# Where the attention's output bias is added: by GpSimd on each image, or by TensorE inside the output projection

## What is computed

```python
def _L0_attn_ref(x, W_qkv, b_qkv, W_o, b_o):
    qkv = x @ W_qkv.T + b_qkv
    ...
    probs = jax.nn.softmax(scores / sqrt(hd), axis=-1)
    out = jnp.einsum('bkhd,bhqk->bqhd', V, probs)
    out = out.reshape(B, S, H)
    return out @ W_o.T + b_o

h = _L0_tok_ref(x, ...)                                   # weighted sum over 4 groups
h = h + _L0_attn_ref(_layernorm(h, axis=-1), W_qkv, b_qkv, W_o, b_o)
h = h + _L0_ffn_ref(_layernorm(h, axis=-1), ...)          # 64 experts, 6 per token, and a shared one
```

## Time and profile before

| | |
|---|---|
| median of 3 runs | 524.37 us (523.19 to 525.21) |
| span of the profiled execution | 527.1 us |
| PE, DVE, ACT, POOL busy over the span | 88%, 63%, 53%, 46% |
| mean granted TensorE clock | 0.953 of full speed |
| POOL's bias add, L397 | 16 of them, 724 to 766 ns each |
| image loop, first to last bias add | 25.0 to 230.3 us |

### The profile page before, as it was taken

How to read it: one execution, slowest core, us unless ns; L and a number is a source line. 1 busy time by engine, 2 the same in 40 slices (tenths; PEclk the granted TensorE clock), 3 DMA queues, 4 the chain that set the end, 5 groups by cost and what they waited for, 6 DMA issues and landing times. The chain is left out here.

```text
span 527.1 us, 11459 instructions
## 1 busy us (share of the span) xinstructions
PE 463.1 (88%) x2974; PEld 351.2 (67%) x2974; DVE 331.5 (63%) x1065; ACT 278.4 (53%) x902; POOL 244.1 (46%) x273
## 2 busy tenths in 40 slices
PE   1687989999999999987648999999999999996796
PEld 1556666766666776755225888888888888873564
DVE  4682658998999999888661443444444444440897
ACT  3285778888777888873201444444445544440000
POOL 1111110566555666666770565665655665661000
PEclk9996989999999999998776999999999999998899
DMA  8999930111111111112224559667678566652997
GB/s 275 348 347 309 299 99 2 61 63 60 62 63 61 62 62 61 63 70 81 101 100 114 181 171 291 203 188 241 200 209 270 165 209 212 205 157 65 415 390 282
DMA packets 56471, 89.82 MB, mean 170 GB/s; under 512 B 7719, under 2 KB 43690, under 8 KB 56400
## 3 DMA queue, kind: packets, MB, share of 16 engines
q1 hardware_dynamic: 44016, 61.62, 37.5%
q0 software_dynamic: 10080, 25.29, 13.6%
q10 hardware_dynamic: 2304, 2.10, 1.1%
HBM read 83.93 MB, written 40.82 MB: 237 GB/s over the span
## 5 line engine op out<-in xcount | busy, mean ns | idle before, releaser
L419 POOL DMA_INDIRECT y_rows<-y,xring x114 | 112.1, 984 | 90.8 <-issue 82.8
L1048 PE MATMUL ps<-wring,prob 128*128 x456 | 119.7, 386 | 0.0
L1009 DVE TENSOR_TENSOR probt<-probt,ps 128x128 f32<-128x128 f32 x114 | 32.8, 288 | 108.6 <-issue 90.7
L1048 PEld LDWEIGHTS ps<-wring,prob 128*128 128x128 f32 x456 | 79.4, 194 | 6.3
L474 ACT ACTIVATE prob<-ps,nmax 128x128 f32<-128x128 f32 x256 | 69.7, 391 | 4.1 <-DVE nmax L706 3.3
L572 ACT COPY prob<-ps 128x256 f32<-128x256 f32 x115 | 42.8, 372 | 48.6 <-PE ps L1279 48.3
L1048 PE MATMUL ps<-wring,probt 128*128 x228 | 68.2, 381 | 0.0
L577 ACT ACTIVATE probt<-ps 128x128 f32<-128x128 f32 x114 | 31.6, 277 | 58.3 <-PE ps L1048 58.3
L1002 DVE TENSOR_SCALAR y<-ps,xring 128x256 f32<-128x256 f32 x114 | 54.6, 479 | 5.8 <-DMA y_rows<-y,xring 4.6
L389 POOL DMA_INDIRECT slot_rows<-row,slot_ix x48 | 50.7, 1056 | 13.7 <-issue 13.4
L389 POOL DMA_INDIRECT slot_rows<-xring,slot_ix x48 | 50.4, 1050 | 14.0 <-issue 13.7
(11 more groups left out here) (173 smaller groups left out, 790.2 us busy)
## 6 DMA issues: line engine op xcount, KB each, us to landing
wring<-wexp SPq DMA_DIRECT2D x115, 384.0 KB
xring<-slot_rows SPq DMA_DIRECT2D x115, 129.0 KB, 2.3
x_sb<-y_rows SPq DMA_DIRECT2D x16, 768.0 KB, 6.3
slot_rows<-pads SPq DMA_DIRECT2D x1, 8256.0 KB, 33.9
x_sb<-x SPq DMA_DIRECT2D x3, 2048.0 KB, 17.8
slot_rows<-pads SPq DMA_DIRECT2D x5, 516.0 KB, 9.6
x_sb<-x SPq DMA_DIRECT2D x4, 512.0 KB, 5.1
out<-h_all ACTq DMA_DIRECT2D x16, 128.0 KB, 6.6
```

The costliest lines, as they stand in the source:

```text
L419: nc.gpsimd.indirect_dma_start(out=y_dram, out_offset=bass.IndirectOffsetOnAxis(ap=xring[:, q, TO_AT:TO_AT + 1].bitcast(I32), axis=0), in_ ...
L1009: nc.vector.tensor_tensor(hm[:, t % 2, :], silu[:, t % 2, :], psS[t % 2][:, INTER:2 * INTER], ALU.mult).then_inc(S("h_ready"), 1)
L1048: return nc.tensor.matmul(*a, **k)
```

## The change

POOL's add per image goes, and with it the semaphore `bias_added` and DVE's wait for it. Once, after `bias_joined`, POOL makes three bf16 terms whose sum is the f32 bias (the first is its rounding, the next two round what is left), multiplies each by a column that is 1 in partition 0, 1 or 2 alone, and adds them up into `bo_rows`, a bf16 tile in which partitions 0, 1 and 2 hold the three terms and all others hold zero. TensorE then starts each projection with one matmul of a matrix of ones and `bo_rows`, which adds the three rows up in every output row, and goes on with the projection's own matmuls in the same accumulation.

```diff
+            split(nc.gpsimd.tensor_copy(bo_term[:, 0, :], bo_sb[:]), 1)
+            split(nc.gpsimd.tensor_tensor(bo_rest[:, 0, :], bo_sb[:], bo_term[:, 0, :], ALU.subtract), 2)
+            split(nc.gpsimd.tensor_copy(bo_term[:, 1, :], bo_rest[:, 0, :]), 3)
+            split(nc.gpsimd.tensor_tensor(bo_rest[:, 1, :], bo_rest[:, 0, :], bo_term[:, 1, :], ALU.subtract), 4)
+            split(nc.gpsimd.tensor_copy(bo_term[:, 2, :], bo_rest[:, 1, :]), 5)
+            for k in range(3):
+                split(nc.gpsimd.tensor_scalar(bo_term[:, k, :], bo_term[:, k, :], c("term")[:, k:k + 1], None,
+                                              ALU.mult), 6 + k)
+            split(nc.gpsimd.tensor_tensor(bo_term[:, 0, :], bo_term[:, 0, :], bo_term[:, 1, :], ALU.add), 9)
+            nc.gpsimd.tensor_tensor(bo_rows[:], bo_term[:, 0, :], bo_term[:, 2, :], ALU.add).then_inc(
+                S("bias_rows"), 1)
...
-                if has(v):
-
-                    pool.wait_ge(S("ln1_done"), v + 1)
-                    nc.gpsimd.tensor_tensor(h_all[:, v, :], h_all[:, v, :], bo_sb[:], ALU.add).then_inc(
-                        S("bias_added"), 1)
...
-                    dve.wait_ge(S("bias_added"), cc + 1)
...
-                    both(psC[:, D:2 * D], lambda k: ont[:, k, :], lambda k: wo_sb[:, k, :]).then_inc(
-                        S("proj_done"), 1)
+                    if cc == 0:
+                        pe.wait_ge(S("bias_rows"), 1)
+                    mm(psC[:, D:2 * D], ones_b[:], bo_rows[:], start=True, stop=False)
+                    for k in range(KT):
+                        last = mm(psC[:, D:2 * D], ont[:, k, :], wo_sb[:, k, :], start=False, stop=k == KT - 1)
+                    last.then_inc(S("proj_done"), 1)
```

More of the change, by code:

```diff
@@ L53 @@
 C_AT = {}
-for _name, _n in (("ident", P), ("causal", P), ("before", P), ("half", 2), ("ebase", E),
+for _name, _n in (("ident", P), ("causal", P), ("before", P), ("half", 2), ("term", 3), ("ebase", E),
                   ("dest", NB * TOPK), ("spill", 1 + NY), ("upto", E), ("tile", NTAB)):
@@ L103, in build @@
         bo_sb = sb("bo_sb", [P, D])
+        bo_rest = sb("bo_rest", [P, 2, D])
+        bo_term = sb("bo_term", [P, 3, D], BF16)
+        bo_rows = sb("bo_rows", [P, D], BF16)
         gate_sb = sb("gate_sb", [P, KT, E])
@@ L223, in build @@
                      "prob_transposed", "probt_ready", "pv_done", "ot_ready", "ot_turned", "c2_chain", "o_ready",
-                     "o_transposed", "ont_ready", "bias_added", "proj_done", "ln_chain", "x2_ready", "var_ready", "root_ready", "var_eps", "half_set",
+                     "o_transposed", "ont_ready", "bias_split", "bias_rows", "proj_done", "ln_chain", "x2_ready", "var_ready", "root_ready", "var_eps", "half_set",
                      "x2_transposed", "x2t_ready", "gate_done", "gate_tanh", "g_chain", "score_read", "sel_ready",
@@ L382, in _, with split @@
             pool.wait_ge(S("bias_joined"), 1)
+            def split(ins, n):
+                ins.then_inc(S("bias_split"), 1)
+                pool.wait_ge(S("bias_split"), n)
+            split(nc.gpsimd.tensor_copy(bo_term[:, 0, :], bo_sb[:]), 1)
[9 more added lines that the diff above has]
+                S("bias_rows"), 1)
             def step(b, par):
-                v, e = b + 1, b - 3
+                e = b - 3
                 def scatter(choices):
@@ L1365 @@
     put("half", p[:, None] // HD % 2 == np.arange(2)[None, :])
+    put("term", p[:, None] == np.arange(3)[None, :])
     put("ebase", np.arange(E)[None, :] * REGION + P + 1)
```

## The result

The changed kernel took 522.86 us (median of 13 runs, 518.38 to 525.21), the kernel before 525.31 us (13 runs, 523.19 to 529.04). The ratio, taken between runs made side by side, is 0.9939, with a 95% interval of 0.9913 to 0.9965. That is 3.2 us less (1.8 to 4.6; the two medians differ by 2.45), a little more than the 0.5% that a measurement can tell. The forecast of 1.1 us less had the sign right and the size too small; the time lies inside the range. In the two profiled executions the span went from 527.1 to 522.1 us.

A forecast was written before the change was run, and what follows sets the result against it. Mid-loop PE and DVE are nearly always busy, and POOL's add holds DVE, delaying ACT's exponential. Terms -1.8 - 0.4 + 0.4 + 0.2 + 0.5 = -1.1 us took 524.37 to 523.3 us; range 520.3 to 526.9.

The forecast's parts named there:

- Where the time goes: Image loop: POOL's add stalls DVE 2.7 us at L731 and L751, making ACT's exponential 3.0 us late over eleven steps.
- 0.21 to 0.58: DVE's stalls per step in us, taken as about as large as the exponential's lateness of 0.20 to 0.78.
- The steady part, -1.8: Eleven loop steps: 3.0 us gained by removing the add, less 1.2 for the new matmul on turn(3).
- second-order gain: PE's 1.6 us of waits for DVE's o_sb in the loop: a quarter, 0.4 us, counted as gained.
- The price of 0.11: Cost in us of each new 256-column matmul on PE ahead of turn(3), bounds 0 and 0.21.
- The start, +0.5: POOL's split from 24.96 us, 6.2 us long, slows DVE's mixing of the third image: 0.5 us lost.
- the start costs its upper bound: Rival: each of four mixing instructions at the start waits out a POOL instruction, 2.6 us lost; 525.4 us, chance 0.15.
- PE's clock falls at the start: Rival: PE idles and returns at half clock in the 10 us behind 30.26, 2.5 us more; 527.9 us, chance 0.12.
- The first three projections, +0.4: Around 59, 75 and 88 us the exponential is not late, so the matmul is pure cost: 0.4 us lost.
- The end, +0.2: At 242.60 us DVE idles for a projection that the matmul delays by 0.11, or 0.22 at half clock: 0.2 lost.
- The rival in which the stall returns whole and the matmul is free: Rival: all of DVE's stalls and PE's o_sb waits come back, matmul hidden in PE's pauses; -3.8 us, 520.6 us, chance 0.18.
- The base: Starting time of 524.37 us for the kernel before, from which the forecast's 1.1 us was taken.

The follow-up runs named there:

- e1: The kernel before without POOL's add and without any output bias, no split and no matmul of ones; ratio to before 0.9950, steps 126.96 us.
- e9: The kernel before with POOL's add moved whole from ahead of the roots to behind them; ratio to before 0.9961, steps 128.82 us.
- e6: The kernel before with each POOL add made twice, the first into a spare tile; ratio to before 1.0032, steps 130.23 us.
- e7: The kernel before with each POOL add replaced by a fill of a spare tile, bias left out; ratio to before 0.9954, steps 128.28 us.
- e2: The kernel before with POOL's add kept and the new matmul put in, on rows of zeros; ratio to before 0.9978, steps 129.35 us.
- e4: The changed kernel with three more matmuls of ones on rows of zeros per projection; ratio to before 1.0027, steps 129.34 us.
- e3: The kernel before with the add kept and POOL's split of the bias made at the start, read by nobody; ratio to before 0.9999, steps 129.46 us.
- e5: The changed kernel with the whole projection, new matmul included, moved behind turn(3); ratio to before 0.9953, steps 126.77 us.
- e10: The changed kernel with DVE's maximum of group 0 made ahead of the choice of experts; ratio to before 0.9928, steps 125.87 us.

## Why the prediction was right or wrong, point by point

- **Where the time goes.** Right. L731 and L751 went back to 225 and 171 ns, the exponential stands 0.48 us behind the copy in all eleven steps, and e1, e9 and e6 show the add as the cause, by way of whom it holds. The stall was not at these two lines alone: "0.21 to 0.58" a step is misread, since in two steps neither is held and the exponential is 0.2 us late by L807. The 3.0 us of lateness, from which the sum was made, had L807's part in it, so the term stood.
- **The steady part, -1.8.** The sum is right, with its second-order gain of 0.4: -2.2 forecast for eleven steps, -2.10 measured over ten. Its terms are not, and that they cancel is in part luck. Taking the add away gave 2.46 us (e1) where I had 3.0, since PE then waited more for `o_sb`; the matmul took back 0.36 (after against e1) where I had 1.2 less 0.4. The account closes within 0.2: lateness -3.0, wait for `o_sb` -0.4, ten matmuls by 0.11 on PE +1.1, in all -2.3. (*Late* counts eleven exponentials; the first, 0.2 us late, stands ahead of the ten steps.) It closes for e1 too (-3.0 + 0.4 = -2.6; -2.46 measured), for e9 (-0.6; -0.60), for e7 (-1.6 + 0.5 = -1.1; -1.14) and for e6 (+0.7; +0.81), and roughly for e2 (-1.4 + 1.1 = -0.3; -0.07). It doesn't for e4: 3.3 - 1.6 = 1.7, and 2.0 was measured. The price of 0.11 was halved from wider matmuls and met exactly. "By 0.1 to 0.2 us a step" was 0.21.
- **The start, +0.5.** Wrong; of the mis-sized terms it moved the forecast most, as those of the steady part cancel. The split lasted 7.7 us, nearer the upper bound of 8.4 than my 6.2, and yet cost 0: I took a price for DVE's mixing from one overlap, but the mixing took 1.84 us beside the casts and two-input steps of the split, as it took 1.87 beside the add. The 0.34 that one overlap had cost was paid before as well, and none came on top. With it the rivals *the start costs its upper bound* and *PE's clock falls at the start* fell: the exponential they needed late came on time (30.28), and e3 gives 0.9999 for the split alone.
- **The first three projections, +0.4.** Too high. The last copies of these images start at 59.83, 75.59 and 88.59 us where they started at 59.79, 75.58 and 88.47: about 0.1 in all, and the roots at 104 are no later. What met the rest of the matmul's cost there I haven't traced.
- **The end, +0.2.** Wrong in kind. In place of 0.2 lost the traces show 1.24 gained, but this is where a stretch of half clock lay in the execution before, and the other traces show it with and without the change. What the change itself costs there these two traces can't show.
- **The rival in which the stall returns whole and the matmul is free, 520.6.** It fell: e2 against e1 and after shows that it is free only while the add's stall covers it, and e4 that it costs 0.11 on PE.
- **The base.** Three runs gave 524.37 us; thirteen gave 525.31. The forecast was a difference of -1.1, the measured one is -3.2 (-1.8 to -4.6). The -2.1 of the steps alone lies in that interval, -1.1 doesn't: the three terms at both ends, +1.1 together, should have been about 0. The 1.1 us between -2.1 and -3.2 is within the interval and needs no cause; I have shown none.

## What to carry to other kernels

Ask of an instruction on GpSimd not how long it takes but which instruction of VectorE stands beside it and who waits for that one: taking the same 0.74 us add away, for 0.11 of matmul, gained 2.1 us in ten steps of one order and 0.4 in another, and a second add, in nine steps of eleven beside instructions that it doesn't hold, cost 0.8. Where two branches end close together, work taken from one alone returns only the difference; find the meeting point, and shorten both (e5 alone gained 0.55 us in the steps, e10 alone 1.45, the two together 4.1). And cut the traces at like events before you compare them: the steps told tenths where the whole span was moved by 1 to 3 us by the clock.

## What the runs showed of the hardware

- **A fill on GpSimd holds VectorE too.** Beside a fill of 0.75 us, which reads nothing, a `tensor_scalar` of 0.17 us took 0.56 (e7); three two-input instructions took 1.52 us beside one, 1.53 without and 1.87 beside an add. A maximum over PSUM was not held by an add (678 ns on average in e6, 679 in before).
- **A multiplication by a pointer on GpSimd is dear in bf16.** 128x256 bf16 took 1.0 us a piece with its wait (3.00 for three in the rows of after above), a cast of the same size 0.40 to 0.47, an addition of two such tiles 0.67. I had put the multiplication at 0.4.
- **The stretches of TensorE's lower clock are not the kernel's alone.** Behind the idle stretch of 42 to 45 us the clock was at 1.2 GHz in every trace, but for a length that differs from trace to trace; where it is long, all that follows is late (before, with 0.50 over 47 to 54 us: roots at 104.24; e2, with 0.63: 101.22; over all traces 100.2 to 104.3).
